# Holding the gathers of the third and fourth batch until a turn has ended

## What is computed

```python
x = x + tanh(g_xattn[0]) * _L0_xattn_ref(ctx_512, _layernorm(x), Wq, Wk, gamma_raw)
x = x + tanh(g_ffn[0])   * _L0_ffn_ref(_layernorm(x), gate_w, w13, w2)      # 64 experts, 8 per token
x = x + tanh(g_xattn[1]) * _L1_xattn_ref(_layernorm(x), ctx_512, ...)       # 16 heads, causal
x = x + tanh(g_ffn[1])   * _L1_ffn_ref(_layernorm(x), ...)                  # 8 experts in full and a shared one
```

## Time and profile before

| | |
|---|---|
| median of 3 runs | 606.56 us (605.2 to 609.0) |
| the profiled execution | 605.59 us |
| its span, first to last instruction | 603.8 us |
| turn 0 (from L699 to the next L699) | 311.6 to 388.1 us |
| turn 1 | 388.1 to 458.4 us |
| turn 2 | 458.4 to 520.1 us |
| turn 3 and what follows | 520.1 to 603.8 us |

### The profile page before, as it was taken

How to read it: one execution, slowest core, us unless ns; L and a number is a source line. 1 busy time by engine, 2 the same in 40 slices (tenths; PEclk the granted TensorE clock), 3 DMA queues, 4 the chain that set the end, 5 groups by cost and what they waited for, 6 DMA issues and landing times.

```text
span 603.8 us, 9222 instructions
## 1 busy us (share of the span) xinstructions
PE 424.7 (70%) x2738; PEld 355.7 (59%) x2738; DVE 344.4 (57%) x1050; ACT 184.5 (31%) x377; POOL 146.4 (24%) x154
## 2 busy tenths in 40 slices
PE   5065543301999999998235735799678988898796
PEld 3043442201998889886124523697468867886686
DVE  2987856297344444333356821488545977482564
ACT  3212300200233333433601412424325262525431
POOL 1307674674000000001776270000730000000000
PEclk9975555555999999998657765799978998899999
DMA  7996221256699999995332030000210000000000
GB/s 266 426 412 280 84 95 69 87 189 230 212 293 320 325 313 323 352 396 187 105 87 80 23 101 19 1 1 3 84 58 17 0 2 0 17 1 3 2 17 18
DMA packets 36693, 82.96 MB, mean 137 GB/s; under 512 B 6000, under 2 KB 16048, under 8 KB 34864
## 3 DMA queue, kind: packets, MB, share of 16 engines
q1 hardware_dynamic: 22800, 55.83, 26.6%
q0 software_dynamic: 6144, 16.79, 8.6%
q10 hardware_dynamic: 7712, 9.90, 4.6%
HBM read 50.44 MB, written 31.92 MB: 136 GB/s over the span
## 4 chain that ended last, share of the span: by engine, by line
PE 51%; DVE 15%; issue 12%; ACT 6%; another core or an unknown queue 5%; POOL 5%; DMA 3%; SPq 2%; DVEq 0%; POOLq 0%; ACTq 0%
PE PS L555 10%; PE PS L565 6%; PE PS L644 5%; POOL slots_in L432 4%; PE PS L542 3%; PE PS L618 3%; PE PS L721 3%; PE PS L657 2%; PE PS L658 2%; PE PS L659 2%; DVE WORK L1060 2%; DVE TOP L1056 2%; PE PS L773 2%; DMA XE<-slots_in 2%
## 5 line engine op out<-in xcount | busy, mean ns | idle before, releaser
L442 POOL DMA_INDIRECT GB<-slots_out,IDXG x64 | 68.7, 1073 | 213.4 <-SPq L365 138.9
L555 PE MATMUL PS<-XTE,WR 128*128 128x128 f32 (+2 forms) x512 | 79.6, 299 | 0.0
L432 POOL DMA_INDIRECT slots_in<-XNA,IDX x64 | 64.9, 1014 | 39.1 <-issue 27.7
L555 PEld LDWEIGHTS PS<-XTE,WR 128*128 128x128 f32 x512 | 70.2, 193 | 0.4 <-ACT XTE L866 0.2
L1245 DVE TENSOR_TENSOR HE<-SGE,PS 128x128 f32<-128x128 f32 (+2 forms) x64 | 19.9, 312 | 69.5 <-ACT SGE L875 66.1
L565 PE MATMUL PS<-WR,HE 128*80 128x256 f32 (+2 forms) x198 | 53.3, 380 | 0.3 <-DVE HE L1245 0.3
L657 PE MATMUL PS<-XH,WGH 128*128 128x256 f32 x160 | 51.6, 322 | 0.0
L866 ACT COPY XTE<-PS 128x256 f32<-128x256 f32 (+2 forms) x64 | 26.3, 410 | 73.0 <-PE PS L542 71.0
L644 PE MATMUL PS<-WD,XW 128*128 128x256 f32 x160 | 43.4, 396 | 5.8 <-DVE TH L1323 5.8
L542 PE MATMUL PS<-CF,XE 80*128 80x80 f32 (+2 forms) x198 | 28.4, 256 | 25.8 <-DMA XE<-slots_in 25.7
L658 PE MATMUL PS<-XL,WGH 128*128 128x256 f32 x160 | 46.2, 289 | 0.0
(11 more groups left out here) (226 smaller groups left out, 824.0 us busy)
## 6 DMA issues: line engine op xcount, KB each, us to landing
WR<-in_wexp SPq DMA_DIRECT2D x64, 384.0 KB
slots_in<-GB SPq DMA_DIRECT2D x12, 1024.0 KB, 18.6
XE<-slots_in SPq DMA_DIRECT2D x24, 160.0 KB, 4.3
slots_out<-OE ACTq DMA_DIRECT2D x24, 160.0 KB, 4.3
XE<-slots_in SPq DMA_DIRECT2D x29, 128.0 KB, 4.4
slots_out<-OE ACTq DMA_DIRECT2D x29, 128.0 KB, 4.8
WGU<-in_wgu SPq DMA_DIRECT2D x1, 2560.0 KB
XE<-slots_in SPq DMA_DIRECT2D x11, 192.0 KB, 3.6
```

The costliest lines, as they stand in the source:

```text
L432: pool.indirect_dma_start(out=xs, out_offset=bass.IndirectOffsetOnAxis(ap=IDX[:, t, j:j + 1], axis=0), in_=XNA[:, t, :], in_offset=None, b ...
L442: pool.indirect_dma_start(out=GB[:, t % BT, j, :], out_offset=None, in_=ys, in_offset=bass.IndirectOffsetOnAxis(ap=IDXG[:, t, j:j + 1], ax ...
L555: last = mm(psGE[place % 2][:, a, 0:cap(place)], W13[:, k, a, :], XTE[:, place % 2, k, 0:cap(place)], start=(k == 0), stop=(k == KC - 1))
```

## The change

Ahead of the gathers of batches 2 and 3, GpSimd waits for `e_gate` to reach b - 1. TensorE raises it once per turn, so batch 2 waits for the router of turn 0, and batch 3 for that of turn 1. The waits on `gb_used` stay.

```diff
             for b in range(B):
+                if b >= 2:
+
+                    pool.wait_ge(S["e_gate"], b - 1)
                 for i in range(BT):
 
                     if b:
                         pool.wait_ge(S["gb_used"], b * BT + i - BT + 1)
                     gather(b * BT + i)
                 if b:
                     pool.wait_ge(S["e_v"], b)
                     nc.gpsimd.tensor_copy(CTB[:, :], CT[:, b * N:(b + 1) * N]).then_inc(S["e_ctx"], 1)
```

## The result

The changed kernel took 611.48 us (median of 4 runs, 607.32 to 614.27) against 605.88 us of the kernel before in the same session (4 runs, 597.33 to 609.0): a ratio of 1.0137, 95% interval 1.0091 to 1.0183. It is **slower by 1.4%**; the forecast was 602.5 us, 0.7% faster. (The ratio and its interval come from the fast runs alone, so they aren't the quotient of the two medians, which is 1.0092.) The profiled execution took 611.56 us, its span 609.8 us, against 605.59 and 603.8.

A forecast was written before the change was run, and what follows sets the result against it. It took TensorE's results, late while gathers run, to bound the kernel. 605.6 - 15.3 (turn 0) - 7.7 (turn 1) + 19.0 (starts of turns 1 and 2) = 601.6 us profiled, 602.5 by the median; range 590 to 614 us.

The forecast's parts named there:

- What bounds the kernel: Turns 0 and 1: TensorE's results come late while gathers run, from about 4.9 us after the first gather in turn 0.
- rival 4: Attention of turns 0 and 1: the lateness is not the gathers' doing, so nothing moves; 606 us, chance 0.08.
- What is removed: Lateness beside the old gather places: 15.3 us in turn 0 and 7.7 us in turn 1, together 23.0 us.
- Turn 0's stretch: From the exponential table's load to the average's copy: 29.0 us before, 13.7 us forecast, so 15.3 us go.
- Turn 1's 7.7 us: From `combine` to the next turn's first transposes: 42.0 us against turn 2's 34.3, the fourth batch's gather cost.
- What is added: Starts of turns 1 and 2: TensorE late beside the moved gathers, 9.5 us per batch, +19.0 us for two.
- rival 3: Turn starts: a full TensorE suffers more, at turn 0's rate from the first gather; 15.6 us per batch, 614.8 us, chance 0.15.
- The sum's -4.0 us: Whole kernel: 605.6 - 15.3 - 7.7 + 19.0 = 601.6 us by the profiled execution.
- both near 77: Lengths in us of turns 1 and 2 in the later profile that would show rival 3 to hold.
- (1): Turn starts are not disturbed at all, so the 23 us are kept; 583.6 us, chance 0.12.
- (2): Only code running for the first time is disturbed: turn 1 pays 9.5 us, turn 2 nothing; 593.1 us, chance 0.15.
- its bound of 15.6 us: Upper bound per batch at a turn's start: turn 0's rate, 2.3 matmuls per us against 7.2, over 23 us.

The follow-up runs named there:

- e3: Kernel before with the gathers of the third and fourth batch left out (other output): 578.00 us against 604.33, ratio 0.9623.
- e10: Changed kernel, each of the 32 late gathers waiting for its own step of TensorE: 575.37 us against 595.97 of the kernel before, ratio 0.9696.
- e13: Changed kernel, GpSimd clearing a scratch tile and waiting for that ahead of each late gather: 581.10 us against 605.14 of the kernel before, ratio 0.9637.
- e4: Changed kernel, late gathers fetching 16 bytes per row instead of 1 KB: 609.42 us against 604.33 of the kernel before, ratio 1.0121.
- e2: Changed kernel, but only the fourth batch's gathers wait for the router: 608.88 us against 604.33 of the kernel before, ratio 1.0124.
- e1: Changed kernel, but only the third batch's gathers wait for the router: 598.70 us against 604.33 of the kernel before, ratio 0.9894.
- e9: Changed kernel run again without alteration: 606.23 us against 595.97 of the kernel before, ratio 1.0207.
- e14: Changed kernel run again without alteration, in another session: 608.04 us against 605.14 of the kernel before, ratio 1.0041.
- e8: Changed kernel, each late gather waiting for its own step of TensorE: 573.59 us against 570.46 of the kernel before, ratio 1.0056.
- e17: Changed kernel, GpSimd clearing a scratch tile and waiting ahead of each late gather: 578.54 us against 569.51 of the kernel before, no ratio.
- e15: Changed kernel, each late gather replaced by a plain GpSimd copy of 128 consecutive rows: 575.79 us against 605.14 of the kernel before, ratio 0.9549.
- e18: Changed kernel run again without alteration: 571.96 us against 569.51 of the kernel before, ratio 1.0051.

## Why the prediction was wrong

**What bounds the kernel: right.** The gathers make TensorE's results come late. e3 (none), e10 and e13 (the same gathers, not in a row) each take it away, and rival 4 is refuted. All this holds for late sessions, the only kind that the prediction's trace could show. Rival 4 rested on the Trainium skill, Trainium Architecture — The Big Picture, section What this means for kernel authors, that the engines' side and the DMA side of SBUF can't contend. e4 agrees with that rule as far as it goes (with 2 GB/s instead of 95 the harm was the same), though no run tests it by itself; but what I drew from it, that gathers then can't slow TensorE's work, does not follow.

**What is removed: right.** Turn 0's stretch came to 13.5 us, forecast 13.7 (15.3 us were to go, 15.4 went; the whole turn lost 15.0). Turn 1's 7.7 us stand against 7.0 in e2 and, by whole turns, the 8.6 us that the prediction also names.

**What is added: the step that failed.** "Two batches: +19.0 us" is the wrong term, 9.5 us per batch. Measured are 77.6 - 61.7 = 16.0 us in turn 2, and in turn 1 76.9 - 61.7 = 15.2, together 31.2 us. That is 12.2 us above the term, and it is the 31.2 us of rival 3. (The 61.7 us are turn 2 of before, used for both; e2's turn 1 without a block took 63.3 us, and against it turn 1 pays 13.6.) The rest of the sum was off by little: 1.9 us less ahead of turn 0, 0.9 us more removed from turn 1, 0.3 less from turn 0, 0.3 more in turn 3. The sum's -4.0 us plus 12.2 - 1.9 - 0.9 + 0.3 + 0.3 makes the measured +6.0.

The term was mis-sized because I took the lateness for a rate: matmuls per us in a disturbed stretch against an undisturbed one. That counts how much work happened to stand in the old places. The runs show delays of single increments: in all ten blocks at a turn's start (after, e1, e2, e4, e9 and e14) the casts of QS start 2.1 to 2.4 us behind the last gather's end, 12 to 14 us behind the shown end of `spread`, however few matmuls there are. What that costs is set by which increments the chain waits for and how much work beside the chain is left. At a turn's start the chain meets `spread`, whose matmuls are shown to end 10 us after the first gather's start, has only one piece of feed-forward beside it, and loses 13 us. In turn 1's second half 7 to 9 us are lost; the late increments there let ScalarE go on at 429.84 and 439.29 us, 14.7 and 5.3 us ahead of the last gather's end, so they were not late to the block's end. Why `spread`'s was, in each of the ten blocks, no run tells. Rival 3 named the size and the side, but its reason ("a full TensorE is bitten harder", turn 0's rate from the first gather on) is the same rate idea and owes its agreement to chance; that it starts with the first gather is wrong, since the queries were still read on time at 376.59 (0.83 us of wait), 5.8 us behind it, and the next piece only at 382.30, with 5.13.

**The rivals.** (1), undisturbed starts, is refuted by turns 1 and 2. (2), only first-run code, is refuted by turn 2, a second pass, which lost as much as turn 1. The mechanism that it leaned on, the fetch of code by DMA (the Trainium skill, Runtime: NRT & Kernel Launch, section Instruction fetch mechanics), was not tested by itself, since that section has the engines fetch in a second pass too. Against it: TensorE had gone on to further matmuls, and both readers of `spread` were released at the same moment. (3) came about, in time, side and "both near 77".

**The signs.** Right were: turn 0 without "remote" waits at its exponentials, blocks that follow a router's end, `combine` without a wait for GB (its first instruction at 414.79 follows VectorE's L1326 at once), ScalarE's waits "remote" from some 5 us on. The lengths of turns 1 and 2 were wrong. That the price at a turn's start was named as the weakest number and its bound of 15.6 us worked out kept the result inside the range; the two "remote" waits in the earlier trace rows were 6.8 and 8.1 us, each for a single signal, which a rate doesn't explain, and should have moved the forecast towards the bound. That the bound itself met the measured price is luck, as said of rival 3.

**Why the change doesn't pay as it stands** in a late session: moved alone, the third batch is 1.1% better (e1), the fourth 1.2% worse (e2). Of the 1.1% a part may be the clock of turn 0, which was high in e1's profile: without it, the third batch takes 15 us away and adds 15. Tied to TensorE's steps (e10) both blocks cost nearly nothing.

## What to carry to other kernels

Price a disturbance by what it holds, not by the mean rate in the stretch where it stands now: find the single waits, ask which signal each was for and when it was released, and lay the same hold over the dependent chain at the new place. Look for the mild place by the slack beside the chain; the start of a turn, where scores wait for one result, was the worst here. And beside moving a harmful block, try to thin it: moved and with a wait ahead of each instruction it brought 3.0% (e10) where moved as a whole it lost 1.4%. Thinned at its old place it was not tried, and in the prompt sessions thinning brought nothing (e8, e17). Run the kernel before next to every experiment, since its own level may change from one session to the next by more than all effects studied.

## What the runs showed of the hardware

- In late sessions, semaphore increments of TensorE come late beside GpSimd's indirect DMAs in a row (one each 1.30 us, 16 in 20.6 us): by 1.4 to 7.7 us in turn 0 of the kernel before, by 12 to 14 us for `spread` at a turn's start, whose readers go on 2.1 to 2.4 us behind the last DMA's end. The same row of gathers ahead of turn 0 delays nothing at 310.8 us, behind 21.6 us in which TensorE stood idle. With 16 bytes per row instead of 1 KB it is the same (e4); with one each 2.34 us (e13), with waits for TensorE between them (e10), or with 16 plain copies in 8.7 us (e15, a shorter block) it is absent. Why, inside the chip, no run tells.
- In prompt sessions the same gathers do nothing of this (e18), and the kernel before takes 569.5 to 571.1 us instead of 596.0 to 605.9. The same recorded chip gave both. What sets it is open. The late traces hold a fifth fewer semaphore increments of the same program (6220 in after, 7775 in e18).
